# Second buffer for a transposed incidence matrix, re-ordered queues and one addition on GpSimd, in a fused hypergraph-convolution and expert-layer kernel

## What is computed

```python
# per graph; xn = layernorm(x)
H  = (adj != 0)                       # 512 x 512, nodes by hyperedges
def conv(u, W, b):                    # 1/deg scalings Dn, Be
    return Dn * (H @ (Be * (H.T @ (u @ W.T)))) + b
h  = layer_norm(relu(conv(xn, W1, b1)))
x1 = x + conv(h, W2, b2) + xn         # second convolution, residuals
# expert layer on x2 = layernorm(x1): top 2 of 4 experts by router logits
comb = sum_e mask[e] * silu(x2 @ expert_w[e] + expert_b[e])
y  = x2 + comb @ out_w + out_b
out = x1 + norm_w * y / rms(y)
```

## Time and profile before

| what | us |
|---|---|
| median of 3 runs | 750.67 (749.53 to 751.47) |
| the profiled execution | 751.47 |
| its span, first to last instruction | 749.9 |
| PE busy | 705.3 (94%) |
| DVE busy | 652.2 (87%) |
| ACT busy | 495.0 (66%) |
| POOL busy | 288.4 (38%) |

### The profile page before, as it was taken

One profiled execution on the slowest core, in us unless ns is written; L12 is line 12 of the kernel. 1 busy time (PEld: TensorE's weight loads), 2 busy tenths in 40 slices (PEclk: granted clock), 3 DMA queues, 4 the chain that ended last, 5 costly groups with the idle time before them and its releaser, 6 DMA issues.

```text
span 749.9 us, 16620 instructions
## 1 busy us (share of the span) xinstructions
PE 705.3 (94%) x5573; PEld 482.4 (64%) x5573; DVE 652.2 (87%) x1569; ACT 495.0 (66%) x971; POOL 288.4 (38%) x670
## 2 busy tenths in 40 slices
PE   4787999999999999999999999999999999999983
PEld 3364584766758486675858577584857768585671
DVE  4878888889898989989898899988899998988776
ACT  4655757667594856758585766858576685847562
POOL 4223334144353525444351434435153453524242
PEclk9988999999999999999999999999999999999997
DMA  8455538376583838657393765738385664727312
GB/s 290 169 110 201 113 89 239 67 225 131 162 178 94 240 64 229 135 172 164 90 245 60 237 122 182 154 105 231 62 247 111 202 134 129 184 64 184 58 29 56
DMA packets 42584, 111.65 MB, mean 149 GB/s; under 512 B 4160, under 2 KB 5312, under 8 KB 42560
## 3 DMA queue, kind: packets, MB, share of 16 engines
q0 software_dynamic: 13536, 41.42, 30.4%
q1 hardware_dynamic: 29024, 69.92, 28.3%
HBM read 69.91 MB, written 16.25 MB: 115 GB/s over the span
## 4 chain that ended last, share of the span: by engine, by line
DVE 29%; PE 26%; DMA 14%; ACT 13%; issue 12%; POOL 2%; SPq 2%; DVEq 0%; POOLq 0%; ACTq 0%
DMA xb<-xn 13%; PE bank L1261 5%; DVE comb L863 4%; PE bank L1263 4%; PE bank L1262 4%; PE bank L1346 4%; PE bank L1347 4%; DVE silu L859 4%; DVE hntl L878 3%; DVE z L867 3%; DVE ybn L980 2%; DVE x L974 2%; DVE h L741 2%; DVE ht L745 2%; ACT xsh L449 2%
## 5 line engine op out<-in xcount | busy, mean ns | idle before, releaser
L1261 PE MATMUL bank<-xth,ewh 128*128 128x512 f16 (+1 forms) x272 | 100.6, 370 | 2.1 <-DVE ewl L782 2.1
L1263 PE MATMUL bank<-xth,ewl 128*128 128x512 f16 (+1 forms) x272 | 100.7, 370 | 0.0
L1262 PE MATMUL bank<-xtl,ewh 128*128 128x512 f16 (+1 forms) x272 | 100.7, 370 | 0.0
L507 ACT ACTIVATE silu<-bank,ebcol,ksc 128x512 f32<-128x512 f32 x120 | 92.1, 769 | 7.3 <-PE bank L1263 7.2
L1261 PE MATMUL bank<-w2h,hnth 128*128 128x256 f16 x256 | 70.7, 276 | 3.3 <-DVE hntl L878 2.6
L1263 PE MATMUL bank<-w2h,hntl 128*128 128x256 f16 x256 | 70.5, 275 | 0.0
L1262 PE MATMUL bank<-w2l,hnth 128*128 128x256 f16 x256 | 70.5, 275 | 0.0
L548 ACT ACTIVATE a1h<-bank,be 128x256 f16<-128x256 f32 x64 | 26.8, 469 | 54.3 <-PE bank L1406 51.0
L654 ACT ACTIVATE uh<-bank,be 128x256 f16<-128x256 f32 x64 | 26.8, 470 | 53.4 <-PE bank L1347 53.4
L525 ACT ACTIVATE hnth<-bank 128x512 f16<-128x512 f32 x64 | 37.9, 592 | 33.3 <-PE bank L1315 33.3
L1405 PE MATMUL bank<-xsh,h 128*128 128x256 f16 x256 | 58.3, 277 | 0.9 <-DVE xsl L764 0.9
(11 more groups left out here) (248 smaller groups left out, 2138.3 us busy)
## 6 DMA issues: line engine op xcount, KB each, us to landing
adjin<-adj SPq DMA_DIRECT2D x16, 1024.0 KB, 5.3
adjtin<-adjt SPq DMA_DIRECT2D x16, 1024.0 KB, 6.2
xin<-x SPq DMA_DIRECT2D x16, 512.0 KB, 4.2
xb<-xn SPq DMA_DIRECT2D x16, 512.0 KB, 8.5
xb<-x POOLq DMA_DIRECT2D x16, 512.0 KB, 8.7
xb<-b POOLq DMA_DIRECT2D x16, 512.0 KB, 5.4
xb<-vadd POOLq DMA_DIRECT2D x16, 512.0 KB, 4.5
out<-x SPq DMA_DIRECT2D x15, 512.0 KB, 6.8
```

What stands on the lines that cost most here:

```text
L507: af(silu[:, i % 4, :], bank[E_BANK[i]][:, :], ACT.Silu, bias=ebcol[:, i:i + 1], scale=ksc[:, 2:3]).then_inc(silu_dn, 1)
L1261: mm(outp, lh, rh, start=first, stop=False)
L1262: mm(outp, lh, rl, start=False, stop=False)
L1263: return mm(outp, ll, rh, start=False, stop=last)
```

## The change

- `ht16` is two buffers, for even and odd graphs. The hardware loop now holds two steps, for graphs g and g + 1 (3 to 14 in 6 rounds). `prep_ht` of graph g + 1 stands on DVE near the end of step g, between `y_part(0)` and the four `ul`, where it stood near the start of step g + 1.
- On SP the copy of `xn` to `xb` is issued first after its wait, then the store of `x1`, then the load of the next `adjt`, which was first of the three.
- ACT: expert half 1 and Tanh stand ahead of the next `xn` tiles; the copy of the mask `mt16` stands ahead of `xsh`.
- PE: tile 3 of h is transposed right after tile 2, ahead of `v_tile(1)`; the router waits for `xtl` in halves.
- The addition of experts 0 and 1 (128 x 1024, f32) goes from DVE to POOL, behind its roots for h; ACT's expert halves 6 and 7 and DVE's next addition wait for it (`half_sum`). The last addition on DVE is made in two halves of columns, so that `cth` can follow by halves, and `vl` of the first tiles stands between the two `ctl`.

The diff, cut:

```diff
-            with eng.Fori(3, N - 1) as g:
-                body(eng, g, conv=True, ffn=True, late=True, prep=True)
-            body(eng, N - 1, conv=True, ffn=True, late=True, prep=False)
+            with eng.Fori(3, N - 2, 2) as g:
+                body(eng, g, 1, conv=True, ffn=True, late=True, prep=True)
+                body(eng, g + 1, 0, conv=True, ffn=True, late=True, prep=True)
+            body(eng, N - 1, 1, conv=True, ffn=True, late=True, prep=False)
@@ SyncE, body @@
+                if ffn:
+                    f = g - 1
+                    sp.wait_ge(x1_dn, 4 * f + 4)
+                if conv:
+                    if not prep:
+                        sp.wait_ge(xn_dn, 4 * g + 4)
+                    sp.dma_start(xb[:, :, :], xn[:, :, :]).then_inc(xn_kept, 16)
+                if ffn:
+                    sp.dma_start(out[f], x1[:, :, :]).then_inc(x1_st, 16)
+                if prep:
                     sp.wait_ge(ht_made, g + 1)
                     sp.dma_start(adjtin[:, :, :], adjt[g + 1].rearrange("(t p) c -> p t c", p=P)).then_inc(adjt_in, 16)
-                if ffn:
-                    f = g - 1
-                    sp.wait_ge(x1_dn, 4 * f + 4)
-                    sp.dma_start(out[f], x1[:, :, :]).then_inc(x1_st, 16)
-                if conv:
-                    sp.wait_ge(xn_dn, 4 * g + 4)
-                    sp.dma_start(xb[:, :, :], xn[:, :, :]).then_inc(xn_kept, 16)
@@ GpSimd @@
+            def add_half(f):
+                gp.wait_ge(comb_st, 7 * f + 2)
+                tt(comb[:, :, :], comb[:, :, :], silu[:, 2:4, :], ALU.add).then_inc(half_sum, 1)
...
                     for t in range(CT):
                         root(hstat, hmv, hve, hrs, hnm, hnb, hrs_st, g, 16, 4 * t, slice(t, t + 1), 4, t + 1)
+                if ffn:
+                    add_half(f)
+                if conv:
...
                     add_b2(g)
@@ ACT, expert and ct_part @@
-                if i >= 4:
-                    act.wait_ge(comb_st, 7 * f + (1 if i < 6 else 3))
+                if 4 <= i < 6:
+                    act.wait_ge(comb_st, 7 * f + 1)
+                if i >= 6:
+                    act.wait_ge(half_sum, f + 1)
...
-                act.wait_ge(comb_st, 7 * f + 7)
+                act.wait_ge(comb_st, 7 * f + 6 + j)
@@ DVE @@
-                TS(ht16[:, :, :], adjtin[:, :, :], 0.0, None, ALU.not_equal).then_inc(ht_made, 1)
+                TS(ht16[odd][:, :, :], adjtin[:, :, :], 0.0, None, ALU.not_equal).then_inc(ht_made, 1)
...
             def combine_sum(f, e):
-                dve.wait_ge(comb_st, 7 * f + 2 * e)
-                TT(comb[:, :, :], comb[:, :, :], silu[:, 2 * (e % 2):2 * (e % 2) + 2, :], ALU.add).then_inc(comb_st, 1)
+                if e == 2:
+                    dve.wait_ge(half_sum, f + 1)
+                dve.wait_ge(comb_st, 7 * f + 2 * e - 1)
+                for s in ((slice(0, C),) if e == 2 else (slice(0, C // 2), slice(C // 2, C))):
+                    TT(comb[:, :, s], comb[:, :, s], silu[:, 2 * (e % 2):2 * (e % 2) + 2, s], ALU.add).then_inc(comb_st, 1)
@@ PE @@
-                    pe.wait_ge(xt_lo, 2 * f + 2)
                     for t in range(CT):
+                        if t % CG == 0:
+                            pe.wait_ge(xt_lo, 2 * f + t // CG + 1)
...
                     v_tile(g, 0)
                     transposed_h(g, 2)
+                    transposed_h(g, 3)
                     v_tile(g, 1)
-                    transposed_h(g, 3)
                     v_tile(g, 2)
```

More of the change, by code:

```diff
@@ L53, in build @@
     CG = 2
-    assert (C, D, DH, NE) == (512, 256, 512, 4)
+    assert (C, D, DH, NE) == (512, 256, 512, 4) and N % 2 == 0
     with ExitStack() as ctx:
@@ L203, in build @@
         a2_lo, v_lo, xt_lo, ct_lo, y_dn = (sem(n) for n in ("a2_lo", "v_lo", "xt_lo", "ct_lo", "y_dn"))
-        comb_st = sem("comb_st")
+        comb_st, half_sum = sem("comb_st"), sem("half_sum")
         last_ob, last_sum, last_y, last_w, last_dn, last_st = (
@@ L221, in steps @@
         def steps(eng, body, tail):
-            body(eng, 0, conv=True, ffn=False, late=False, prep=True)
-            body(eng, 1, conv=True, ffn=True, late=False, prep=True)
-            body(eng, 2, conv=True, ffn=True, late=True, prep=True)
-            with eng.Fori(3, N - 1) as g:
-                body(eng, g, conv=True, ffn=True, late=True, prep=True)
-            body(eng, N - 1, conv=True, ffn=True, late=True, prep=False)
+            body(eng, 0, 0, conv=True, ffn=False, late=False, prep=True)
+            body(eng, 1, 1, conv=True, ffn=True, late=False, prep=True)
+            body(eng, 2, 0, conv=True, ffn=True, late=True, prep=True)
+            with eng.Fori(3, N - 2, 2) as g:
+                body(eng, g, 1, conv=True, ffn=True, late=True, prep=True)
+                body(eng, g + 1, 0, conv=True, ffn=True, late=True, prep=True)
+            body(eng, N - 1, 1, conv=True, ffn=True, late=True, prep=False)
             tail(eng)
@@ L254, in _, with body @@
                 sp.dma_start(dst, src).then_inc(c_in, 16)
-            def body(sp, g, conv, ffn, late, prep):
+            def body(sp, g, odd, conv, ffn, late, prep):
                 if prep:
@@ L381, in add_yf, with body @@
                 gp.dma_start(out[q][:, s, :], yf[:, s, :], accum_op=ALU.add).then_inc(out_st, 16)
+            def add_half(f):
+                gp.wait_ge(comb_st, 7 * f + 2)
+                tt(comb[:, :, :], comb[:, :, :], silu[:, 2:4, :], ALU.add).then_inc(half_sum, 1)
             prep_x(0, again=False)
-            def body(gp, g, conv, ffn, late, prep):
+            def body(gp, g, odd, conv, ffn, late, prep):
                 f, q = g - 1, g - 2
@@ L556, in x2_part, with body @@
                        scale=yrs[:, t:t + 1]).then_inc(x2_dn, 1)
-            def body(act, g, conv, ffn, late, prep):
+            def body(act, g, odd, conv, ffn, late, prep):
                 f = g - 1
@@ L588, in body @@
                     expert(act, f, 0)
+                if ffn:
+                    expert(act, f, 1)
+                    act.wait_ge(arg_dn, f + 1)
+                    af(th[:, :, :], arg[:, :, :], ACT.Tanh).then_inc(th_dn, 1)
                 if prep and ffn:
                     prep_x(g + 1, (0, 1))
-                if ffn:
-                    act.wait_ge(arg_dn, f + 1)
-                    af(th[:, :, :], arg[:, :, :], ACT.Tanh).then_inc(th_dn, 1)
-                    expert(act, f, 1)
                 if prep and ffn:
@@ L992, in degrees, with body @@
                 v.reciprocal(be[:, :], dmax[:, :]).then_inc(be_dn, 1)
-            def body(dve, g, conv, ffn, late, prep):
+            def body(dve, g, odd, conv, ffn, late, prep):
                 f, q = g - 1, g - 2
@@ L1365, in turned_x2, with a2_half @@
                 ins.then_inc(xt_rdy, 1)
-            def a2_half(g, half, ffn):
+            def a2_half(g, odd, half, ffn):
                 pe.wait_ge(a1_lo, 4 * g + CG * half + CG)
@@ L1374, in a2_half @@
                     for k in range(CG * half, CG * half + CG):
-                        mm(bank[A2_BANK[d]][:, :], a1h[:, k, P * d:P * d + P], ht16[:, k, :],
+                        mm(bank[A2_BANK[d]][:, :], a1h[:, k, P * d:P * d + P], ht16[odd][:, k, :],
                            start=(k == 0), stop=False)
-                        ins = mm(bank[A2_BANK[d]][:, :], a1l[:, k, P * d:P * d + P], ht16[:, k, :],
+                        ins = mm(bank[A2_BANK[d]][:, :], a1l[:, k, P * d:P * d + P], ht16[odd][:, k, :],
                                  start=False, stop=(k == CT - 1))
@@ L1380, in a2_half, with body @@
                         ins.then_inc(a2_rdy, 1)
-            def body(pe, g, conv, ffn, late, prep):
+            def body(pe, g, odd, conv, ffn, late, prep):
                 f = g - 1
@@ L1417, in body @@
                         for k in range(CT):
-                            ins = mm(bank[D_BANK][:, 4 * t:4 * t + 4], ht16[:, k, P * t:P * t + P], wcur[:, k, :],
+                            ins = mm(bank[D_BANK][:, 4 * t:4 * t + 4], ht16[odd][:, k, P * t:P * t + P], wcur[:, k, :],
                                      start=(k == 0), stop=(k == CT - 1))
```

32 lines of the change are left out of this document (17 added, 15 removed).

## The result

| | before | after |
|---|---|---|
| median, us | 750.9 (749.53 to 751.47) | 737.95 (737.60 to 738.52) |
| ratio | | 0.983 (95%: 0.9811 to 0.985) |
| profiled execution, span | 751.47, 749.9 | 737.89, 736.4 |

The forecast was 738.7. The page of the kernel after: span, busy time by engine, two rows of the queues that bring the code, and the chain by engine.

What follows compares the result with a forecast made beforehand. PE was taken to bound the kernel at 43.38 us a graph. Gains of 9.4 (graphs 3 to 14), 1.7 (graph 2), 1.0 (graph 1), less 0.15 (graph 0), together 12.0, gave 738.7 us from 750.67; range 734.5 to 748.

Steps and rivals of the forecast that it cites:

- Ceiling: In graphs 3 to 14, a PE without gaps has a period of 42.5 us, so at most 10.6 us to gain.
- Each gap has its own cure: PE's three gaps in graph 7, 0.84 us in sum, each closed by one edit on PE or ACT.
- Router, 0.22: PE's gap between A2 and the router, 0.22 us, goes when the router waits for `xtl` by halves.
- Mask, 0.29: PE's gap before the mask row, 0.29 us, goes when ACT does the mask copy and Tanh first.
- `v_tile(3)`, 0.33: PE's gap before `v_tile(3)`, 0.33 us, goes when tile 3 of h is transposed early.
- The comparison a graph ahead: DVE's 1.20 us comparison of `ht` moves before the `ul`, fits within 0.1, booked at nothing in the loop.
- `half_sum`: POOL's addition takes 2.6 us, nothing gained or lost; rival, chance 0.08: it takes 3.9, costing 1.0 a graph, 753.7 us.
- the point that decides: In graph 7, `half_sum` must be there by about 352.6; it was expected at 352.3.
- Code fetched again: Rival, chance 0.09: the two-step loop does not fit, each of 5 backward branches waits some 1.9 us, 748 us.
- Small waits take half back: Rival, chance 0.20: PE arrives earlier and waits for `ctl`, `hntl` or `ul`, 0.45 us a graph, 745 us.
- Graph 1: The comparison's move takes 1.20 us off the path to `ewl` in graph 1; 1.0 us booked as gain.
- Start and graph 0: In graph 0 the comparison's new place before the `ul` is tighter; 0.15 us booked as loss.

Runs made afterwards that it cites:

- three_edits: The kernel before with only the router's wait in halves, tile 3 of h transposed early on PE, and ACT's new order: 745.37 us.
- four_edits: three_edits with DVE making `hntl` of tile 3 ahead of the whole last addition of the experts: 749.21 us.
- five_edits: four_edits with last addition and `ctl` in halves; still one `ht` buffer compared at step start, one-step loop, first addition on DVE, SP's old order: 743.21 us.
- ht_at_start_one_wait: The changed kernel with the comparison of `ht` back at the step's start and the router waiting once for both halves of `xtl`: 740.59 us.
- no_addition_on_pool: The changed kernel with the addition of experts 0 and 1 back on DVE, behind the second weighing: 738.45 us.
- no_tile3: The changed kernel with tile 3 of h transposed behind `v_tile(1)` on PE again: 755.40 us.
- ewh_early: The changed kernel with `ewh` made by ACT at the end of graph 0's step and `ewl` by DVE ahead of `xtl`: 733.37 us.

## Why the prediction was right, and where it was not

**Ceiling: right.** A period of 42.5 for a PE without gaps, worked out from one graph of the kernel before, against 42.48 measured. The 0.1 a graph kept back was not needed; that is 12 x 0.1 = 1.2 of the 1.4 by which the loop beat its term, and graph 2 gave all of its 2.4.

**Each gap has its own cure: wrong.** This is the step of the working that failed, though the sum hides it. The prediction read three gaps with three releasers and gave each to one edit. The runs show:

- *Router, 0.22.* Cured by the halves or by the comparison's move; in the changed kernel either can be left out alone. Undone together they cost 0.26 a graph (42.745 against 42.483), 0.22 of it at the router.
- *Mask, 0.29.* Cured by ACT's order or by the comparison's move.
- *`v_tile(3)`, 0.33.* Not cured by PE's early tile 3 (0.41 stays in three_edits). The prediction's 356.5 for `hntl` of tile 3 already had it right behind tile 2's, which is DVE's new order and not PE's. It needs DVE's `hntl` ahead of the last addition too, and then the addition's lateness appears as 0.65 at the output product (four_edits), until the rest of the reordering brings it to 0.11 (five_edits).

From 43.38 the path is 43.02, 43.24, 42.71, 42.48: not a sum of terms, but at the end of the step one gap pushed along a chain. All three places hang on DVE's queue, the mask by way of ACT's copy, and what most likely closes the last of it is time taken off the start of DVE's step.

**The comparison a graph ahead: booked at nothing in the loop, worth about 0.26 where it is the only cure.** "It fits within 0.1" was right for its new place; what the step missed is what leaves the old one. 1.2 us less ahead of `a1l`, `xtl` and the weighing makes it a second cure for two gaps. It is the likeliest source of five_edits' missing 0.23 as well. The addition on POOL and SP's order, which that run lacks too, cost nothing when undone from the change, and ht_at_start_one_wait, with the addition on POOL, has the pair of `hntl` as late as five_edits has it (29.61 and 29.62, against 29.34). The loop of two steps can hardly move it, but the move alone on top of five_edits was not run.

**`half_sum`: right, the rival properly priced.** 2.35 instead of 2.6, and a delay of 1.0 costs 0.46 and not 0.7, since the point that decides lay 0.5 behind the addition's end, where 0.3 was forecast; the 0.25 by which the addition was quicker is the difference. The step on the root, from 0.96 to 0.19, came out too, and it is back at 0.96 in no_addition_on_pool. The Trainium skill's "SBUF — State Buffer", section "Who interferes with whom", says that a VectorE instruction with two SBUF inputs contends with a GpSimd instruction that reads SBUF, and one with a single such input does not. The traces agree with both halves: 0.96 against 0.19 for the first; for the second the 2.35, which begins while DVE idles and ends beside `hntl` and the weighing, whose other operand is in PSUM.

**Code fetched again: did not happen.** 17 pieces on q8 instead of 14, for a source with one more step body (the page does not name the engine; the prediction took this queue for PE's), and 14 instead of 10 on q14. A body is about 3 pieces by the prediction's count, so the doubled loop was brought in once; fetched in each of 6 rounds it would have been over 30. No graph of the loop is longer than another by more than 0.01. By the window that "Runtime: NRT & Kernel Launch", section "Instruction fetch mechanics", of the Trainium skill gives for TensorE, 2048 instructions, the doubled loop, some 1380 matmuls and weight loads by the stretches above, fits, and the trace agrees.

**Small waits take half back: did not happen**, though three_edits and five_edits show that the margins were as thin as feared: 0.10 at `v_tile(2)` in both. What widened them was the comparison's move, which the rival had not counted.

**Graph 1: 2.0, not 1.0: the term gave 0.7, and the clock came on top.** The stretches give 1.9; by the starts of the degree products graph 1 took 51.14 before and 49.13 after. `ewl` begins 11.82 after the graph's start instead of 12.54, so the term that the prediction booked at 1.0 gave 0.7; against ht_at_start_one_wait `ewl` is 1.0 earlier. PE's longer wait for `ewl` (2.46 where it was 2.08) is no loss, since PE only arrives earlier. The slow stretch behind the wait is shorter: before, the products from 70.32 to 75.82 lost 2.7 in it, after they lose 1.7, which makes 1.0. The closed gap at `v_tile(3)` gives the last 0.27. The clock's 1.0 can't be put down to the change: the slow stretch falls differently from trace to trace, and in three_edits, where `ewl` begins at 12.86, it lies in A2 and graph 1 takes 48.75.

**Start and graph 0: -1.4, not -0.15, cause open, but it is not the new work.** From the first A2 product of graph 0 to the start of graph 1 it took 34.91 before and 34.66 after, and the last part, from the first product with `vh` in graph 0 that waits for `vl`, with the comparison ahead of the `ul`, 7.26 and 7.27. So the booked 0.15 did not show. The loss is all ahead of A2:

```profile
20.47 0.39 PE L1375 MATMUL bank<-ht,a1h 128*128 128x512 f16 x1
```
```profile
22.17 0.39 PE L1392 MATMUL bank<-ht_even,a1h 128*128 128x512 f16 x1
```

From the start of graph 0 that is 7.61 before and 9.60 after, partly a longer stretch at the low clock (products of 256 columns 0.21 apart up to 20.5 instead of 17.8), partly a longer wait of PE for DVE's `mags` (a gap of 1.0 instead of 0.3). The order of the work there is the same in all the kernels, and the other twelve took 8.42 to 10.43; three_edits, for one, 8.68. Why the kernel before, in its one trace, was quicker than all of them stays open.

The total was thus right by a good ceiling and by some luck: the wrong assignment of the gaps could not show, since the change held two cures for two of them and both halves of the third, and the errors of the single terms (+1.4, +0.7, +0.9, -1.25, -0.2) in part cancelled.

## What to carry to other kernels

Gaps on the bounding engine that all come from one other engine's queue are not additive: closing one lets the next late product show. Price them together as a ceiling (the period of a graph without gaps), and say which *order of the producer's queue* reaches it, before giving each gap an edit. Two engines that pass tiles on need their orders changed in step: one alone can lose, as in no_tile3. Even both together can lose until what stands behind them on the producer is fitted in as well, as in four_edits. And a long setup operation on the path of an early graph costs its wait and the clock after it: moving `ewl` gave a third as much as all the rest, for two moved calls.

## What was not expected of the hardware

- After PE had waited 2.46 for `ewl`, its clock was at 1.2 GHz for 3.4 us from 0.65 after the restart, and cost 1.7. Without the wait (ewh_early) the same stretch ran at 2.4 GHz throughout. In ht_at_start_one_wait the slow stretch stood in the A2 products, after PE had waited 1.14 for `ht_odd` and 0.54 for `a1l`, and the 1.75 that PE waited for `ewl` later was followed by none.
- POOL's addition of 128 x 1024 in f32 took 2.35 or 2.36 in all 15 graphs; an addition of 128 x 512 took 1.04 with both operands the same buffer, and 1.27 in the tail with two. VectorE is held up by such an addition too: beside POOL's, two `yf` of the tail took 1.93, and the next two, with POOL idle, 1.29.
- The busy share says little near the limit: PE at 94% before and 95% after, for 1.7% of the time.
